# Two graph layers on one core: fewer maxima chunks, more differences on POOL, edge flags on DVE, the output bias in PE's sums

## Chip, cores and metric

The kernel runs on one core of one Trainium2 chip. The metric is the time of one execution of the whole program in microseconds (us). Before the change three runs gave a median of 1157.24 us (1155.14 to 1157.57).

## What is computed

x is (64 graphs, 128 nodes, 128 channels), adj is (64, 128, 128). Two residual layers follow each other; cut to what matters:

```python
h = relu(layernorm(x))
D = abs(h[:, :, None, :] - h[:, None, :, :])            # every pair of nodes of a graph
p = einsum('bijc,oc->bijo', D, W1) + b1                  # 64 products for each pair
p = leaky((p - mean(p)) / sqrt(var(p) + EPS) * g1 + be1) # statistics over all graphs and pairs
s = where(adj > 0, einsum('bijo,uo->biju', p, W2)[..., 0] + b2, NEG)
y = (softmax(s) @ h) @ Wg.T + bg
y = leaky((y - mean(y)) / sqrt(var(y) + EPS) * gg + beg) # again over all graphs
x = x + concatenate([h, y], axis=2) @ Wt.T + bt
h = relu(layernorm(x)); v = h @ W
e = leaky(v @ a[:128] + (v @ a[128:]).T, 0.2)
x = x + elu(softmax(where(adj > 0, e, NEG), axis=1) @ v)
```

## The kernel before

The pair differences need statistics over all graphs before they can be used, so the kernel goes through them twice. The 64 graphs are 32 couples of two, 16 quads of four. D is symmetric: 64 shifts of a graph against itself cover all pairs. A couple has 64 shifts in 8 chunks m = 0 to 7 of 8 shifts (PER = 8, CHUNKS = 256). Every engine has its program written out by hand, as a loop over a step n (chunk number) with offsets that say at which n each piece of work stands; an engine executes in that order and waits on semaphores.

**First pass** (about 30 to 660 us). For each chunk a tile `diff` of 128 x 2048 is made (5 slots, so chunk n waits for the product of chunk n-5). There are three sorts. In MAXED chunks (m = 0, 3, 6) DVE writes the maximum of the two nodes (`subtract` at L291, from PSUM and `h_ext`) and PE subtracts the sum of the two with twelve extra bf16 matmuls (`products_by_max`, L751 and L755): no absolute value is needed. In POOLED chunks (m = 1, 4, 7) POOL subtracts (L291), in the others (2, 5) DVE does; then ACT takes the absolute value (`absolute`, L567) and PE multiplies (`products`, L741). The products lie in one of three PSUM pairs of banks. KEPT chunks (all but m = 2, 7) are copied by ACT to SBUF (`take`) and stored in DRAM by SP's queue. The statistics of COUNTED chunks are made by DVE (`count`, bn_stats, L1040), from SBUF for kept ones and from PSUM for m = 2 and 7. For TAKEN chunks (m = 0, 5) ACT makes them: the copy with a running sum (L582) and a square from PSUM (L586). ACT's order in step n is: `normalise` and the other layer-norm pieces of the next quad (once a quad, at NORM_AT = 3, EXT_AT = 5, HIGH_AT = 7, MID_AT = 10), then `absolute(n)`, then `take(n-2)`. PE's transposes of the next quad stand at TURN_AT = 4, ahead of chunk 4 of the quad (L713); ACT's `turn_out` (L536) needs them. PE's `node_products` (NODE_AT = 6, L731) feed ACT's `high` (L541), whose rest DVE splits in `rest` and `low` (L1005, two inputs in SBUF). POOL also turns adj into flags `no_edge` (`edges`, L448, two halves for each couple).

**Second pass** (665 to 1003 us). SP loads the kept products into 10 slots (`load_kept`), chunks m = 2 and 7 are made again by DVE (`again`: L291 and a bit mask, L1055) and PE; ACT applies scale, bias and leaky relu (`activate`, L644), and PE sums the 64 products to scores (L845). Beside this runs the attention of quad j, at steps 16 j + offset: EVAC 24 `take_rows` (DVE), DIST_T 25 transposes (PE), TURN 27 `take_turned` (DVE), `store_skew`, `load_half` (DMAs through DRAM on POOL's queue, L470, L476) and `sum_half` (POOL, L480), SUM 41 `att_sum` (PE, L874, L875), SCORES 43 `att_scores` (DVE), EXP 45 (ACT, L649), NORM 48 `att_norm` (DVE, L1160), TURN_P 49 (PE), COPY 51 (DVE), MIX 53 (PE, L889), and Y 56 `att_y` (DVE: bias from PSUM, L1170, then bn_stats, L1171). `att_sum(j)` waits in `at_zero` for the y of quad j-1.

**The end of the second pass.** The last two quads' attention runs out with no chunks beside it. In this stretch SP loads x again (`load_x`, L383), POOL adds the bias of the output (`x_and_bias`, L485: six tiles between `load_half(15)` and `sum_half(15)`, ten behind it), and PE and DVE make the part of the output that comes from h for the first PRE = 6 quads (`outputs_of_x`, L799, at MADE_AT; `fold_x`, L1177, at FOLD_AT). Then come the statistics of y and the **last stage** (1050 us on), 16 quads in a software pipeline, with `outputs` (L915, L916) first.

Of the kernel before, what the change touches and what calls it, by code (L numbers as in the profile page):

```python
# [9 lines left out]
BF16 = mybir.dt.bfloat16  # L10
# [30 lines left out]
MAXED = (0, 3, 6)  # L41
POOLED = (1, 4, 7)
PLAIN = (2, 7)
COUNTED = (1, 2, 3, 4, 6, 7)
# [16 lines left out]
SUM_PARTS = (0, 16, 29, COUPLES)  # L61
# [25 lines left out]
def two_layers(nc, x, adj, adj_t, w1_tt, wg_t, wt1_t, wt2_t, l1_w, l1_wt, cols, bt_rows,  # L87
# [8 lines left out]
    with ExitStack() as ctx:  # L96
# [15 lines left out]
        bt_sb = sb("bt_sb", [128, C])  # L112
        ident = sb("ident", [128, 128])
# [34 lines left out]
        def by_graph(t):  # L148
# [9 lines left out]

        ln_st = sb("ln_st", [128, B, 6])
# [8 lines left out]
        sums_dump = sb("sums_dump", [128, NCOUNTED * 4])  # L168
# [39 lines left out]
        skew_stored = [sem("skew_stored0"), sem("skew_stored1")]  # L208
        skew_cleared = [sem("skew_cleared0"), sem("skew_cleared1")]
# [4 lines left out]
        weighted, weighted_ready = sem("weighted"), sem("weighted_ready")  # L214
# [4 lines left out]
        bt_ready, x_bt, y_act, o_mm, x1_ready, dve_f, var2_ready, rstd2_ready, scale2_ready, h2_ready, h2_turned, \  # L219
            h2t_ready = (sem(n) for n in (  # L220
                "bt_ready", "x_bt", "y_act", "o_mm", "x1_ready", "dve_f", "var2_ready", "rstd2_ready",
# [73 lines left out]
        EVAC, DIST_T, TURN, SUM, SCORES, EXP, NORM, TURN_P, COPY, MIX, Y = 24, 25, 27, 41, 43, 45, 48, 49, 51, 53, 56  # L295
        STORE_SKEW, LOAD_HALF = 30, 36
# [7 lines left out]
        def mix_at(n):  # L304
            u, r = divmod(2 * n, 3)
            return EARLY_MIX + u if r < 2 and 0 <= u < NQ - EARLY_MIX else None

# [11 lines left out]
        FOLD_AT = tuple(QCH * j + step for j in (NQ - 2, NQ - 1) for step in (SCORES, NORM, COPY))  # L319
        MADE_AT = (264, 266, 270, 274, 277, 284)  # L320
# [26 lines left out]
        def _(sp):  # L347
# [3 lines left out]
            def load_adj(v):  # L351

                if v >= 2:
                    sp.wait_ge(edges_set, 2 * (v - 1))
                sp.dma_start(adj_sb[v % 2], (adj_n, adj_tn)[v % 2][:, quad(v // 2), :]).then_inc(adj_in[v % 2], 16)
# [22 lines left out]
            def load_x(j):  # L378
                if j < PRE:
                    sp.wait_ge(prod2_ready, NPLAIN)  # L380
                else:
                    sp.wait_ge(scored, CHUNKS // 2)
                sp.dma_start(X[j], x_n[:, quad(j), :]).then_inc(x_in2[j], 16)  # L383

            AHEAD = LRING
            FIRST_LOADS = (LRING - 1) // len(KEPT) * PER + KEPT[(LRING - 1) % len(KEPT)]
            for n in range(CHUNKS + TAIL + AHEAD):
                if n < CHUNKS and n % PER in KEPT:
                    load_kept(n)
# [6 lines left out]
                if n == CHUNKS + AHEAD - 1:  # L396
                    for q in range(NQ):
                        load_x(q)
# [12 lines left out]
        def _(pool):  # L411
# [3 lines left out]
            nc.gpsimd.memset(skew_init[:, :], 0.0)  # L415
            nc.gpsimd.memset(sums_st[:, :, :], 0.0)
# [28 lines left out]
            def edges(v, half):  # L445
                pool.wait_ge(adj_in[v % 2], 16 * (v // 2 + 1))
                b = QUAD * (v // 2) + 2 * half
                nc.gpsimd.tensor_scalar(no_edge[v % 2][:, b:b + 2, :], adj_sb[v % 2][:, 2 * half:2 * half + 2, :], 0.0, None,  # L448
                                        ALU.is_le).then_inc(edges_set, 1)

            for n in range(CHUNKS):
# [4 lines left out]
                if n % PER in (2, 5):  # L456
                    edges(n // PER, n % PER // 5)
# [4 lines left out]
            def store_skew(j):  # L462
# [5 lines left out]
                whole = skew_dram[j % 2]  # L468
                dst = bass.AP(whole.tensor, whole.offset + 1, [[EXT + 1, N], [N * EXT, QUAD], [1, DIST]])
                nc.gpsimd.dma_start(dst, s_turn[:, :, :]).then_inc(skew_stored[j % 2], 16)  # L470
# [7 lines left out]
            def sum_half(j):  # L478
                pool.wait_ge(half_in, 16 * (j + 1))
                nc.gpsimd.tensor_tensor(s_half[:, :, 0:EXT - N], s_half[:, :, 0:EXT - N], s_half[:, :, N:EXT],  # L480
                                        ALU.add).then_inc(half_summed, 1)

            def x_and_bias(j):
# [819 lines left out]
```

## Time and profile before

| | |
|---|---|
| median of three runs | 1157.24 us (1155.14 to 1157.57) |
| the profiled execution's own time | 1156.38 us |
| its span in the trace | 1154.6 us |
| busy, share of the span | PE 91%, DVE 91%, ACT 86%, POOL 50% |
| first pass | to about 660 us |
| second pass | 665 to 1003 us |
| run-out of the attention | to about 1050 us |
| last stage | to 1154.6 us |

Busy times of an engine are unions: an instruction's last tenth of a microsecond overlaps the next one's start, so the distance of two starts is a little shorter than the duration shown. "Idle before" names what ended the wait of the engine. PEclk is the granted clock, 1.00 being 2.4 GHz and 0.50 being 1.2 GHz.

### The profile page before, as it was taken

Reading aid. Unit: us, or ns where it says so; the run is one execution under the profiler, and the core shown is the slowest. Engines: PE = TensorE matmul, PEld = TensorE weight load, DVE = VectorE, ACT = ScalarE, POOL = GpSimd, SP = SyncE. Lnnn points to the kernel's source line nnn. Section 1 sums busy time; section 2 is a strip of 40 time slices with the busy share of each in tenths; the row PEclk is TensorE's granted clock in tenths of the full one; section 3 lists DMA queues with packets and bytes.
Section 4 is the critical chain, followed back from the end, with each engine's and each line's share of the span. In section 5 each row is a group of like instructions: output and inputs, shape, how many; then the busy total and the mean of one; then the engine's idle time right before and its main releaser. Section 6 shows DMA issues by size and latency. Waiting matters only on the chain.

```text
span 1154.6 us, 17648 instructions
## 1 busy us (share of the span) xinstructions
PE 1054.3 (91%) x6470; PEld 473.9 (41%) x6470; DVE 1047.1 (91%) x1389; ACT 993.4 (86%) x1252; POOL 580.9 (50%) x332
## 2 busy tenths in 40 slices
PE   3999999999999999999999999999999999835997
PEld 1333333333333433333333452333333333335997
DVE  5999999999999999999999867999999999755887
ACT  4889998999999999999999889989899898703987
POOL 6587768767777877686777400111212221171330
PEclk9999999999999999999999989999999999976999
DMA  6444444444443444444444688999899999730012
GB/s 178 165 156 184 172 158 169 184 166 188 166 192 146 174 185 171 159 185 184 171 168 176 235 321 292 335 332 339 319 339 329 321 334 324 222 92 1 29 47 74
DMA packets 97269, 233.32 MB, mean 202 GB/s; under 512 B 8096, under 2 KB 44448, under 8 KB 97184
## 3 DMA queue, kind: packets, MB, share of 16 engines
q1 hardware_dynamic: 93040, 223.11, 53.2%
q0 software_dynamic: 2560, 8.39, 2.1%
q8 instruction: 52, 0.85, 0.3%
q10 hardware_dynamic: 1584, 0.69, 0.3%
q14 instruction: 33, 0.27, 0.1%
HBM read 124.43 MB, written 107.74 MB: 201 GB/s over the span
## 4 chain that ended last, share of the span: by engine, by line
PE 47%; DVE 37%; issue 7%; ACT 7%; DMA 1%; POOL 1%; ACTq 0%; DVEq 0%; POOLq 0%
PE psum L741 16%; DVE store L291 16%; PE psum L751 10%; PE psum L755 7%; DVE plain_st L1040 5%; DVE store L1055 4%; ACT store L567 3%; PE psum L932 1%; PE psum L916 1%; PE psum L933 1%; DVE early L1160 1%; PE psum L731 1%; PE psum L950 1%; PE psum L941 1%; PE psum L713 1%
## 5 line engine op out<-in xcount | busy, mean ns | idle before, releaser
L291 POOL TENSOR_TENSOR store<-h_ext 128x2048 f32<-128x2048 f32 (+1 forms) x96 | 386.6, 4029 | 119.5 <-PE psum L741 115.6
L741 PE MATMUL psum<-store,w1tt_sb 128*64 128x512 f32 x1792 | 421.1, 598 | 17.7 <-ACT store L567 17.5
L291 DVE TENSOR_TENSOR store<-psum,h_ext 128x2048 f32<-128x2048 f32 x160 | 364.1, 2275 | 0.7 <-ACT h_ext L537 0.7
L567 ACT ACTIVATE store<-store 128x2048 f32<-128x2048 f32 x160 | 305.1, 1932 | 6.2 <-POOL store L291 3.1
L644 ACT ACTIVATE store<-store,st 128x1024 f32<-128x1024 f32 x192 | 226.5, 1241 | 0.0
L741 PEld LDWEIGHTS psum<-store,w1tt_sb 128*64 128x64 f32 x1792 | 122.0, 136 | 252.8 <-issue 236.2
L751 PE MATMUL psum<-store,w_twice 128*64 128x512 f32 x768 | 200.6, 599 | 4.9 <-DVE early L1005 3.5
L291 DVE TENSOR_TENSOR store<-h_ext 128x2048 f32<-128x2048 f32 x64 | 146.2, 2285 | 17.9 <-PE psum L741 17.9
L1040 DVE BATCH_NORM_STATS2 plain_st<-store 128x6 f32<-128x512 f32 x256 | 160.6, 678 | 0.0
L755 PE MATMUL psum<-early 128*64 128x512 bf16 x1152 | 158.0, 380 | 0.0
L845 PE MATMUL psum<-store,w_rows 128*32 128x512 f32 x1024 | 134.3, 607 | 3.2 <-ACT store L644 3.2
L579 ACT COPY store<-psum 128x1024 f32<-128x1024 f32 x128 | 128.7, 1024 | 4.8 <-PE psum L741 4.8
L755 PEld LDWEIGHTS psum<-early 128*64 128x64 bf16 x1152 | 69.1, 110 | 133.0 <-issue 114.6
L1040 DVE BATCH_NORM_STATS2 plain_st<-psum 128x6 f32<-128x512 f32 x128 | 82.5, 686 | 17.9 <-PE psum L741 17.9
L1055 DVE TENSOR_SCALAR store<-store 128x2048 int32<-128x2048 int32 x64 | 81.3, 1270 | 2.2
L751 PEld LDWEIGHTS psum<-store,w_twice 128*64 128x64 f32 x768 | 53.0, 137 | 73.1 <-issue 29.1
L644 ACT ACTIVATE store<-psum,st 128x1024 f32<-128x1024 f32 x64 | 76.7, 1199 | 0.3 <-PE psum L741 0.3
L470 POOL DMA_DIRECT2D score_skew<-early x16 | 12.9, 805 | 120.2 <-DVE early L1133 120.2
L586 ACT ACTIVATE psum<-psum,st 128x1024 f32<-128x1024 f32 x64 | 69.8, 1091 | 1.1 <-DVE st L1084 1.1
L649 ACT ACTIVATE early<-early 128x512 f32<-128x512 f32 x16 | 10.1, 630 | 65.2 <-DVE early L1153 65.2
L582 ACT ACTIVATE store<-psum 128x1024 f32<-128x1024 f32 x64 | 65.4, 1022 | 0.2
L480 POOL TENSOR_TENSOR early<-early 128x256 f32<-128x256 f32 x16 | 17.1, 1070 | 92.5 <-DMA early<-score_skew 92.5
(155 smaller groups left out, 1195.6 us busy)
## 6 DMA issues: line engine op xcount, KB each, us to landing
kept_products<-store SPq DMA_DIRECT2D x192, 512.0 KB, 2.7
store<-kept_products SPq DMA_DIRECT2D x192, 512.0 KB, 6.0
early<-score_skew POOLq DMA_DIRECT2D x16, 384.0 KB, 6.8
early<-adj SPq DMA_DIRECT2D x16, 256.0 KB, 3.6
early<-adj_t SPq DMA_DIRECT2D x16, 256.0 KB, 3.5
store<-x SPq DMA_DIRECT2D x16, 256.0 KB, 5.6
out<-early SPq DMA_DIRECT2D x16, 256.0 KB, 2.3
score_skew<-early POOLq DMA_DIRECT2D x16, 128.0 KB, 6.0
```

Of the source, the lines that this page charges most:

```text
L291: return engine.tensor_tensor(t[:, :, 0:steps, :], nodes.unsqueeze(2).broadcast_to([C, 2, steps, N]), windows(h_ext[:, 2 * c, :], STEP * m ...
L567: nc.scalar.activation(t, t, ACT.Abs).then_inc(abs_ready, 1)
L579: nc.scalar.copy(kept[k % ZRING], tile).then_inc(kept_ready, 1)
L582: nc.scalar.activation(kept[k % ZRING], tile, ACT.Identity, accum_out=sum_p[:, t:t + 1])\
L586: nc.scalar.activation(tile, tile, ACT.Square, bias=sc(0), accum_out=sum_m[:, t:t + 1])\
L644: nc.scalar.activation(dst, src, ACT.Prelu, bias=sc(14), scale=sc(12), alpha=SLOPE0)\
L741: last = nc.tensor.matmul(t[MID * g:MID * g + MID, b, :], w1tt_sb[:, 0:MID], diff[slot][:, g, b * BANK:b * BANK + BANK], start=True, stop= ...
L751: nc.tensor.matmul(t[MID * g:MID * g + MID, b, :], w1_twice[:, :], diff[n % SLOTS][:, g, b * BANK:b * BANK + BANK], start=True, stop=False)
L755: last = nc.tensor.matmul(t[MID * g:MID * g + MID, b, :], y_parts[:, c % 4, s, MID * g:MID * g + MID], pair_nodes[:, k, b * BANK:b * BANK ...
L845: last = nc.tensor.matmul(score[j % 2][32 * q:32 * q + 32, :], w2_rows[:, r, :], src[:, b * BANK:b * BANK + BANK], start=(r == 0), stop=(r ...
L1040: last = nc.vector.bn_stats(plain_st[:, p, t, :], src[:, t, :])
L1055: nc.vector.tensor_scalar(bits, bits, 0x7FFFFFFF, None, ALU.bitwise_and).then_inc(diff2_ready, 1)
```

## The change

- First pass: MAXED is (0, 4), POOLED (1, 3, 5, 7), DVE's differences are m = 2 and 6, COUNTED is all but m = 0, so TAKEN is m = 0 alone. The offsets of the layer-norm pieces stay.
- `edges` goes from POOL (two halves) to DVE (one instruction a couple, ahead of the work of step m = 3).
- The output bias: DVE splits bt - 1 into three bf16 rows once, at step 32 (`split_bias`, eight small instructions), and PE adds it with one bf16 matmul of 512 columns for each quad (`biases`). POOL's sixteen `x_and_bias` are gone.
- x is loaded again by ACT's queue: eight issues between `activate(254)` and `activate(255)`, eight behind a wait for the last scores.
- PRE goes from 6 to 8; `outputs_of_x` stands at 257, 258, 266, 267, 270, 273, 277, 282, `fold_x` at new steps.
- `att_y` is cut in two: ACT adds the bias (`y_to_nodes`, step 56), DVE makes bn_stats (`y_sums`, step 57).
- The skewed store and load of quads 14 and 15 are issued by SP instead of POOL.
- The sums of the statistics (`sums`) take 224 instead of 192 chunks' values, cut at couples 16 and 27 instead of 16 and 29.

```diff
-MAXED = (0, 3, 6)
-POOLED = (1, 4, 7)
+MAXED = (0, 4)
+POOLED = (1, 3, 5, 7)
 PLAIN = (2, 7)
-COUNTED = (1, 2, 3, 4, 6, 7)
+COUNTED = (1, 2, 3, 4, 5, 6, 7)
...
-SUM_PARTS = (0, 16, 29, COUPLES)
+SUM_PARTS = (0, 16, 27, COUPLES)
...
-        FOLD_AT = tuple(QCH * j + step for j in (NQ - 2, NQ - 1) for step in (SCORES, NORM, COPY))
-        MADE_AT = (264, 266, 270, 274, 277, 284)
+        FOLD_AT = [QCH * (NQ - 1) + TURN] * 2 + [QCH * (NQ - 2) + step for step in (SCORES + 1, NORM, COPY, Y_SUMS)] + \
+            [QCH * (NQ - 1) + step for step in (SCORES, NORM)]
+        MADE_AT = (257, 258, 266, 267, 270, 273, 277, 282)
...
+            for j in range(BY_POOL, NQ):
+                store_skew(j)
+                load_half(j)
...
             for n in range(CHUNKS):
                 if n in POWER_AT:
                     deviation(POWER_AT.index(n))
                 if n % PER in POOLED:
                     differences(n)
-                if n % PER in (2, 5):
-                    edges(n // PER, n % PER // 5)
...
-                if j == NQ - 1:
-                    pool.wait_ge(bt_ready, 1)
-                    for q in range(PRE):
-                        x_and_bias(q)
                 sum_half(j)
...
-            for q in range(PRE, NQ):
-                x_and_bias(q)
...
+            def y_to_nodes(j):
+                act.wait_ge(out_mm, j + 1)
+                nc.scalar.activation(h_nat[:, quad(j), :], att[0], ACT.Identity, bias=BG).then_inc(y_out, 1)
...
                 if n < CHUNKS:
                     activate(n)
+                if n == CHUNKS - 2:
+                    act.wait_ge(prod2_ready, NPLAIN)
+                    for q in range(8):
+                        load_x(q)
+                if n == CHUNKS - 1:
+                    act.wait_ge(scored, CHUNKS // 2)
+                    for q in range(8, NQ):
+                        load_x(q)
...
+            def biases(o):
+                nc.tensor.matmul(o, ones_bf[:, :], bt_rows3[:, :].unsqueeze(1).broadcast_to([128, QUAD, C]),
+                                 start=True, stop=False)
...
-                for s, step in ((s_masked, SCORES), (y_ready, Y)):
+                for s, step in ((s_masked, SCORES), (y_out, Y)):
...
+            def edges(v):
+                dve.wait_ge(adj_in[v % 2], 16 * (v // 2 + 1))
+                nc.vector.tensor_scalar(no_edge[v % 2][:, quad(v // 2), :], adj_sb[v % 2], 0.0, None, ALU.is_le)\
+                  .then_inc(edges_set, 1)
...
+                in_turn(nc.vector.tensor_scalar(bt_sb[:, :], bt_sb[:, :], -1.0, None, ALU.add))
+                for k in range(2):
+                    in_turn(nc.vector.tensor_copy(bt_high[:, k, :], bt_sb[:, :]))
+                    in_turn(nc.vector.tensor_tensor(bt_sb[:, :], bt_sb[:, :], bt_high[:, k, :], ALU.subtract))
+                nc.vector.tensor_copy(bt_rows3[0:1, :], bt_high[0:1, 0, :])
+                nc.vector.tensor_copy(bt_rows3[32:33, :], bt_high[32:33, 1, :])
+                nc.vector.tensor_copy(bt_rows3[64:65, :], bt_sb[64:65, :]).then_inc(bt_ready, 1)
...
+                if n == 2 * QCH:
+                    split_bias()
+                if n < CHUNKS and n % PER == 3:
+                    edges(n // PER)
...
-            def att_y(j):
-                dve.wait_ge(out_mm, j + 1)
-                y = h_nat[:, quad(j), :]
-                linked(nc.vector.tensor_scalar(y, att[0], BG, None, ALU.add))
-                nc.vector.bn_stats(bst[:, j, :], y.rearrange("p b n -> p (b n)")).then_inc(y_ready, 1)
-
-            dve.wait_ge(edges_set, 2 * COUPLES)
+            def y_sums(j):
+                dve.wait_ge(y_out, j + 1)
+                nc.vector.bn_stats(bst[:, j, :], h_nat[:, quad(j), :].rearrange("p b n -> p (b n)")).then_inc(y_ready, 1)
```

## Rows read from the trace of the kernel before

**Rows 1.** Stretches: busy us (instructions) of PE, PEld, DVE, ACT, POOL; PEclk; DMA share, GB/s.
```profile
100.00:500.00 400.00, 388.18 (x2184) 151.27 (x2182) 387.70 (x419) 375.63 (x430) 296.39 (x143) 1.00 0.45 174
...
800.00:1000.00 200.00, 187.61 (x1236) 67.58 (x1232) 194.97 (x213) 179.11 (x165) 41.35 (x37) 1.00 0.90 320
1000.00:1050.00 50.00, 22.32 (x148) 17.83 (x144) 27.05 (x40) 4.25 (x6) 24.30 (x22) 0.75 0.39 103
```

**Rows 2.** One POOL instruction of each couple's chunk 7: count, first and last start.
```profile
L289 POOL TENSOR_TENSOR store<-h_ext x32: 453/457/461, 31.8 to 645.9; 128x128 f32<-128x128 f32 x32
```

**Rows 3.** Groups by line in 100 to 500 us.
```profile
L291 POOL TENSOR_TENSOR store<-h_ext 128x2048 f32<-128x2048 f32 (+1 forms) x61 | 245.9, 4032 | 75.6 <-PE psum L741 75.6
...
L1040 DVE BATCH_NORM_STATS2 plain_st<-store 128x6 f32<-128x512 f32 x163 | 102.3, 678 | 0.0
```

**Rows 4.** Timeline of the first pass: start, duration, engine, line.
```profile
299.95 1.03 PE L751 MATMUL psum<-store,w_twice 128*64 128x512 f32 x4
...
301.17 1.02 ACT L582 ACTIVATE store<-psum 128x1024 f32<-128x1024 f32 x1
...
302.96 1.89 PE L741 MATMUL psum<-store,w1tt_sb 128*64 128x512 f32 x8
...
303.25 1.02 ACT L579 COPY store<-psum 128x1024 f32<-128x1024 f32 x1
...
304.14 3.74 ACT L567 ACTIVATE store<-store 128x2048 f32<-128x2048 f32 x2
...
314.23 0.66 PE L713 MATMUL psum<-ident,h_nat 128*128 128x128 f32 x4
...
314.93 0.59 ACT L536 COPY h_ext<-psum 128x512 f32<-128x512 f32 x1 [0.58 <-PE psum L713]
```

**Rows 5.** Waits of ACT in 100 to 500 us: total, times, longest.
```profile
ACT early L541 <- PE psum L731: 13.4, 10, 1.3
ACT h_ext L536 <- PE psum L713: 4.6, 8, 0.6
```

**Rows 6.** DVE beside POOL: one stretch of the timeline, and two lines' durations.
```profile
376.21 8.01 POOL L291 TENSOR_TENSOR store<-h_ext 128x1792 f32<-128x1792 f32 x2
...
378.76 1.38 DVE L1005 TENSOR_TENSOR early<-y_rest,early 128x256 bf16<-128x256 f32 x1
...
L1005 DVE TENSOR_TENSOR early<-y_rest,early x16: 400/408/1383, 22.0 to 613.6; 128x256 bf16<-128x256 f32 x16
...
L1055 DVE TENSOR_SCALAR store<-store x64: 1226/1227/1737, 655.4 to 991.4; 128x2048 int32<-128x2048 int32 x64
```

**Rows 7.** DVE's bias of y in the second pass: durations, first and last start.
```profile
L1170 DVE TENSOR_SCALAR h_nat<-psum,col x16: 739/744/751, 743.6 to 1046.2; 128x512 f32<-128x512 f32 x16
```

**Rows 8.** SP's loads of x: duration of the issue, min/median/max in ns.
```profile
L383 SPq DMA_DIRECT2D store<-x x16: 383/832/1791, 1000.6 to 1013.1; - x16
```

**Rows 9.** Timeline from the last activation to the second batch-norm.
```profile
1001.55 1.19 ACT L644 ACTIVATE store<-psum,st 128x1024 f32<-128x1024 f32 x1
...
1010.22 0.78 POOL L470 DMA_DIRECT2D score_skew<-early  x1 [4.30 <-DVE early L1133]
...
1010.89 1.95 PE L799 MATMUL psum<-wt_sb,h_ext 128*128 128x128 f32 x16
...
1013.26 0.63 ACT L649 ACTIVATE early<-early 128x512 f32<-128x512 f32 x1 [10.52 <-DVE early L1153]
...
1017.88 0.76 POOL L476 DMA_DIRECT2D early<-score_skew  x1 [6.88 <-issue]
1018.65 7.35 POOL L485 TENSOR_TENSOR store<-store,bt_sb 128x512 f32<-128x512 f32 x6
...
1021.55 5.00 DVE L1160 TENSOR_TENSOR early<-early,rows 128x512 f32<-128x512 f32 x1
...
1034.28 0.46 PE L874 MATMUL psum<-early,ident 128*128 128x128 f32 x2 [1.67 <-DVE bst L1171]
...
1037.78 2.14 DVE L1153 TENSOR_TENSOR early<-early,rows 128x512 f32<-128x512 f32 x1
```

More of the change, by code:

```diff
@@ L208, in two_layers @@
         skew_stored = [sem("skew_stored0"), sem("skew_stored1")]
+        late_stored, late_in = ([sem(f"{t}{n}") for n in range(2)] for t in ("late_stored", "late_in"))
         skew_cleared = [sem("skew_cleared0"), sem("skew_cleared1")]
@@ L306, in mix_at, with skewed @@
             return EARLY_MIX + u if r < 2 and 0 <= u < NQ - EARLY_MIX else None
+        BY_POOL = NQ - 2
+        def skewed(j):
+            whole = skew_dram[j % 2]
+            return bass.AP(whole.tensor, whole.offset + 1, [[EXT + 1, N], [N * EXT, QUAD], [1, DIST]])
         def quad_at(n, step):
@@ L376, in load_kept, with store_skew, load_half @@
                 sp.dma_start(loaded[k % LRING], kept_dram[k, :, :]).then_inc(kept_in[k % LRING], 16)
[L378 to L385, printed above, removed]
+            def store_skew(j):
+                sp.wait_ge(turn_ready, j + 1)
+                sp.wait_ge(half_in, 16 * (j - 1))
+                sp.dma_start(skewed(j), s_turn[:, :, :]).then_inc(late_stored[j - BY_POOL], 16)
+            def load_half(j):
+                sp.wait_ge(late_stored[j - BY_POOL], 16)
+                sp.wait_ge(s_sum, j)
+                sp.dma_start(s_half[:, :, :], skew_dram[j % 2].rearrange("b (i j) -> i b j", j=EXT))\
+                  .then_inc(late_in[j - BY_POOL], 16)
             FIRST_LOADS = (LRING - 1) // len(KEPT) * PER + KEPT[(LRING - 1) % len(KEPT)]
-            for n in range(CHUNKS + TAIL + AHEAD):
-                if n < CHUNKS and n % PER in KEPT:
+            for n in range(CHUNKS):
+                if n % PER in KEPT:
                     load_kept(n)
@@ L597, in sums @@
                                                      (1, ACT.Identity, dict(scale=256.0)))):
-                    at = 4 * first + (1024 if k == 1 else 0)
-                    dump = (sums_dump[:, :] if k == 2 else tiles(28, 4))[:, at:at + 4 * (last - first)]
+                    dump = sums_dump[k][part][:, 0:4 * (last - first)]
                     done = nc.scalar.activation(dump, counted_part(of)[:, 4 * first:4 * last], how,
@@ L653, in _ @@
                     activate(n)
+                if n == CHUNKS - 2:
[6 more added lines that the diff above has]
+                        load_x(q)
                 if mix_at(n) is not None:
                     nodes_out(mix_at(n))
[L656 to L658 removed]
+                for step, do in ((Y, y_to_nodes), (EXP, exps)):
+                    j = quad_at(n, step)
+                    if j is not None:
+                        do(j)
             def bn_leaky(j):
@@ L1181, in _ @@
                     again(n + LEAD_DIFF)
-                for step, do in ((Y, att_y), (EVAC, take_rows), (TURN, take_turned), (SCORES, att_scores),
+                for step, do in ((Y_SUMS, y_sums), (EVAC, take_rows), (TURN, take_turned), (SCORES, att_scores),
                                  (NORM, att_norm), (COPY, att_copy)):
@@ L1186, in _ @@
                         do(j)
-                if n in FOLD_AT:
-                    fold_x(FOLD_AT.index(n))
+                for k in range(PRE):
+                    if n == FOLD_AT[k]:
+                        fold_x(k)
             done[0] = 0
```

83 lines of the change are left out of this document (47 added, 36 removed).

## The prediction

> **What bounds the kernel now.** I read the busy times by stretch first, then, in the first pass, the period of a couple, the groups, ACT's waits and a piece of the timeline; in the second pass DVE's lines; behind it the timeline. From 100 to 500 us DVE is busy for 387.7 us of 400, PE for 388.2, ACT for 375.6, POOL for 296.4 [rows 1]. The same instruction of POOL comes every (645.9 - 31.8) / 31 = 19.81 us [rows 2]: that is a couple; a quad takes 39.6 us, and 400 us hold 10.1 quads. A quad so has 38.4 us of DVE, 38.4 of PE, 37.2 of ACT, 29.3 of POOL. Three engines are within 6% of the bound, so taking work from one helps only as far as the next, and ACT is that next one. In the second pass (800 to 1000 us) DVE is busy for 97.5%, PE for 94%, ACT for 89.6% [rows 1]: DVE ends it. In the run-out (1000 to 1050 us) no engine is busy for more than 27 of 50 us: a chain of waits.
>
> **First pass: PE.** Two maxima chunks a quad become chunks of differences. A maxima chunk starts at 299.95 and the next one at 302.96, 3.0 us; a chunk of differences takes up to 1.9 [rows 4]. PE loses at least 2.2 us a quad and bounds nothing any more.
>
> **DVE.** Per couple it loses one difference (2.2) and gets one pair of bn_stats (2 x 0.61, as 102.3 us for 163 give 0.63 [rows 3]) and one `edges`. No row has this instruction on DVE. Bounds: a quarter of the 2048-wide one, 0.31, and the 512-wide one from PSUM, 0.74 [rows 6, 7]; I take 0.5. 19.2 - 2.2 + 1.2 + 0.5 = 18.7 us a couple, 37.4 a quad.
>
> **POOL.** Four differences of 4.0 us (245.9 / 61 [rows 3]) and about 0.4 more for chunk 7, 33.5 us a quad: free, unless a difference starts late.
>
> **ACT.** Per quad two absolute values more, 2 x 1.87 (3.74 for two [rows 4]); two chunks are copied only: from L582's start at 301.17 to L579's at 303.25 are 2.08 us, a copy takes 0.9 (303.25 to 304.14) [rows 4], so 2 x 1.2 less. 37.2 + 3.7 - 2.4 = 38.5 us. To this comes a wait that the new order makes. `turn_out` stands ahead of `absolute(5)` and needs the transposes that PE does behind chunk 3. Before, ACT had `absolute(4)` to do meanwhile and waited 0.58 us [rows 4], in all 4.6 us in 400 [rows 5]. Now m = 4 is a maxima chunk and m = 2 isn't kept, so between `absolute(3)` and `turn_out` ACT has only the copy of chunk 1, 0.9 us, while PE does chunk 3, which waits for that absolute value (1.8), and 0.70 us from the transposes' start to ACT's [rows 4]: a wait of 1.6 us in each quad that no lead of PE can hide. The wait for `node_products` (13.4 us in 400 [rows 5]) should mostly go: two absolute values of ACT now stand behind PE's chunk 5 by my working of the order. So a quad takes at least 38.5 + 1.6 = 40.1 us, and I take 40.3, with 0.2 for the waits that remain: 0.7 more than 39.6, in 15.5 quads **+11 us**. From both sides: 39.7 (all small waits gone, the added wait half hidden) is +1, and 40.9 (0.8 of the old waits kept) is +20.
>
> **DVE and POOL together.** `low` (L1005, both inputs in SBUF) takes 0.41 us, but 1.38 where it meets a running difference of POOL: at 378.76 it lasts until 380.14, shortly behind the end (379.9) of the first of POOL's two differences [rows 6]. `split_bias` has two such subtractions and other small instructions beside them. If each subtraction and copy waits for the rest of a difference of 4.0 us, half of it on average, that is 4 x 2 = 8 us of DVE once, of which the other engines' lead hides most: **+2** (0 to +8). `edges` has one input in SBUF; a mask with one input (L1055) takes 1.23 and at most 1.74 in a pass in which POOL does little [rows 6], so I let `edges` wait only where DVE has room for it (18.7 of 20.2 us a couple).
>
> The Trainium skill (SBUF — State Buffer, Who interferes with whom) says that `tensor_scalar` from SBUF to SBUF can also take the port pair that POOL uses, and that the later of the two then waits for the whole instruction. The trace agrees for two inputs and shows no certain case for one. By that rule the second rival below is the likelier course; by the rows alone the sum stands.
>
> **Second pass.** The bias of y leaves DVE: 16 x 0.744 us [rows 7], of which some twelve lie where DVE is the bound, 9 us. ACT gets as much (0.6 to 0.74 each) and goes from 89.6% of a quad of 21.1 us (338 us for sixteen) to 96% of one of 20.3: nearly a bound. Its waits leave DVE part of the gain: **-7** (-9 to -1).
>
> **The run-out.** First a loss: eight DMA issues now stand between `activate(254)` and `activate(255)`, which started at 1001.55 [rows 9], with the last scores behind it. An issue of this load took 0.38 to 1.79 us on SP, median 0.83, most of that under a full queue [rows 8]; for the first eight I take 0.55: +4.4 (3.1 to 6.7). Two `outputs_of_x` of 1.0 us (1.95 for two [rows 9]) plus a bias matmul now stand ahead of quad 13's end; ACT's bias beside `take_rows` gives about as much back. So quad 14's exponential ends at 1013.9 + 4.4, about 1018.3, instead of 1013.9 [rows 9]. Then the gain. Before, DVE sat behind `fold_x(0)`, this behind POOL's `x_and_bias`, this behind the issue at 1017.88, which waited 7.7 us for the store of 1010.22 [rows 9]; and the normalising L1160 then took 5.00 us beside POOL's six, until 1026.55 [rows 9]. Now three folds (0.7 each) and 1.6 us of normalising follow: 1021.5. On to `att_sum(15)` were 7.7 us, to 1034.28 [rows 9]; without the four `outputs_of_x` between them at half clock about 5: 1026.5. The half of quad 15 is stored at about 1014 and, with 7.7 us for the store as before, 4.8 for the load and 0.7 for the sum, there at 1027.2; without the queue of x earlier. So 1027 against 1034.3, -7.3; L1153's 2.14 us beside POOL [rows 9] are 0.7 again, -1.4: **-9** (-14 to -3).
>
> **Last stage.** Two quads less of eight matmuls (0.12 us each, as sixteen in 1.95 [rows 9]), eight bias matmuls more: 0. `sums`: 0. POOL makes one pair table less ahead of the first chunks: 0 to -1.
>
> **Sum.** The profiled execution has 1156.4 us; + 11 + 2 - 7 - 9 = 1153.4. The median of the runs is 0.9 above it, so 1154.
>
> **Rivals.** *The shared wait* (slower): in each couple `edges` meets a difference of POOL that has just begun. Its place is step m = 3; its price is up to 4.0 us for DVE, and it decides from the point where it exceeds DVE's room, 20.2 - 18.7 = 1.5 us. At 4.0 in each second couple, 16 x 2.5 = 40; at an average rest of 2.0 in all, 32 x 0.5 = 16. I take +22: 1176. For it: L1005's 1.38, and POOL now has a difference on for 83% of the time. Against it: L1005 met one seldom (median 0.408 [rows 6]), as the order puts it into POOL's pauses. Chance 0.22.
> *The ACT wait doesn't come* or old waits shrink as much (39.6 us a quad, PE's room helps all): first pass 0 instead of +11, so 1143. For it: PE gets 2.2 us of air; against it: chunk 3 needs `absolute(3)`. Chance 0.17.
> *The end gives less*: ACT becomes the bound of the second pass (-2) and the eight issues cost 6.7 and more, the skews come no sooner (-4): 1164. Chance 0.13.
> *Forecast*, 1154 (1146 to 1162): 0.48.
>
> **Numbers.** About 0.2% (2.3 us) is what a measurement can tell. Of the forecast's 0.48, 0.28 lies more than 2.3 under 1157.2, 0.15 within, 0.05 above; of the ACT rival's 0.17, 0.15 is faster and 0.02 within; of the other two's 0.35, 0.32 is slower and 0.03 within. Faster 0.43, same 0.20, slower 0.37. The range leaves out 2 in 10: 1142 to 1179, from the ACT rival to the shared wait's mean with its spread.
>
> **What would show it.** The pass-1 instruction of POOL in chunk 7 comes every 20.15 us; L536's counterpart on ACT waits about 1.6 us in each quad; ACT is busy 96% there, PE under 90%. `edges` lasts 0.3 to 0.7 us; durations of 2 to 4 us there mean the shared wait. The y line on DVE is gone and DVE's share falls from 97.5%. Eight issues between the last two activations take 4 to 5 us; from the first of them to `att_sum(15)` pass about 25.5 us, where from the same place (1001.55) to 1034.28 it was 32.7. A first pass of 19.8 us a couple or less makes the forecast wrong, as does a run-out that isn't shorter.

## The result, and the profile after

The changed kernel takes 1188.39 us, the median of four runs (1187.35 to 1190.48), against 1156.19 (1154.60 to 1157.57) for the kernel before beside it: a ratio of 1.0276, interval 1.0251 to 1.0300. It is 32 us slower, and outside the range of 1142 to 1179. The profiled execution took 1187.45 us, its span is 1185.5.

The stretches below are divided by these landmarks, which both kernels have: `turn_out`'s copies in the first pass (ACT, one a quad, L537 now), the first and last but one activation of the second pass, and the first batch-norm output `bn_leaky`.

| stretch | before | after | difference |
|---|---|---|---|
| start to the second quad's copy | 36.54 | 44.58 | +8.0 |
| from there to the sixteenth copy, 14 quads | 554.97 | 589.90 | +34.9 |
| to the first activation of the second pass | 71.95 | 76.40 | +4.4 |
| to `activate(254)` | 336.96 | 329.16 | -7.8 |
| run-out, to `bn_leaky` | 49.33 | 40.41 | -8.9 |
| last stage | 104.85 | 105.05 | +0.2 |

So the three stretches behind the first pass came out as forecast in their sums, and the first pass with its two ends lost 47 us instead of 13. Busy times by stretch in the kernel after (columns as in [rows 1]; the third row has the length of one whole quad, the last is 2 us at the start of a chunk 3):

```profile
100.00:500.00 400.00, 353.17 (x1852) 137.58 (x1850) 378.68 (x450) 369.14 (x369) 330.92 (x118) 0.98 0.43 167
800.00:1000.00 200.00, 190.83 (x1264) 68.59 (x1260) 195.45 (x208) 188.25 (x177) 39.57 (x37) 1.00 0.94 336
258.54:298.82 40.28, 35.97 (x194) 14.08 (x192) 37.04 (x42) 38.02 (x38) 33.66 (x13) 1.00 0.44 170
338.00:340.00 2.00, 2.00 (x7) 0.60 (x4) 2.00 (x3) 0.29 (x1) 2.00 (x1) 0.50 0.44 180
```

In the first pass no engine is as full as PE and DVE were in [rows 1]. The POOL instruction of [rows 2], `edges` (L1075) and `low` (L1035) by source line, then ACT's waits from 100 to 500 us:

```profile
L293 POOL TENSOR_TENSOR store<-h_ext x32: 449/460/656, 39.0 to 688.3; 128x128 f32<-128x128 f32 x32
L1075 DVE TENSOR_SCALAR no_edge<-early x32: 400/414/4526, 35.7 to 684.1; 128x512 uint8<-128x512 int32 x32
L1035 DVE TENSOR_TENSOR early<-y_rest,early x16: 417/668/2945, 23.1 to 656.0; 128x256 bf16<-128x256 f32 x16
```

```profile
PE psum L762 <- ACT store L568: 46.5, 31, 3.7
ACT h_ext L537 <- PE psum L734: 21.0, 9, 3.5
```

The couple now comes every (688.3 - 39.0) / 31 = 20.95 us. The wait at `turn_out` was 4.6 us in 400 [rows 5] and is 21.0. The timeline shows what it consists of, once in a regular quad, the length that recurs most (first two lines: its chunk 3 and its copy), and once in a long one:

```profile
297.26 1.94 PE L762 MATMUL psum<-store,w1tt_sb 128*64 128x512 f32 x8 [2.29 <-ACT store L568]
...
299.82 0.59 ACT L537 COPY h_ext<-psum 128x512 f32<-128x512 f32 x1 [1.81 <-PE psum L734]
...
335.49 1.90 ACT L568 ACTIVATE store<-store 128x2048 f32<-128x2048 f32 x1
337.29 1.00 ACT L580 COPY store<-psum 128x1024 f32<-128x1024 f32 x1
337.54 3.54 PE L762 MATMUL psum<-store,w1tt_sb 128*64 128x512 f32 x8 [2.29 <-ACT store L568]
341.01 0.70 PE L734 MATMUL psum<-ident,h_nat 128*128 128x128 f32 x4
341.74 0.59 ACT L537 COPY h_ext<-psum 128x512 f32<-128x512 f32 x1 [3.46 <-PE psum L734]
```

Six of the fourteen quads take 40.28 or 40.29 us and have the wait of 1.81. Three take 41.9: there PE stood idle for 2.29 us for `absolute(3)`, the granted clock from 338 to 340 us is 0.50, so 1.2 GHz, and the eight matmuls of chunk 3 take 3.54 us instead of the 1.9 of [rows 4]. ACT waits 3.46 us. In the regular quads PE stands idle there for the same 2.29 us (first line), and the clock stays at 1.00. The other five take 41.1 to 48.2; the half clock lies in some of them too (in the one that ends at 219.26, behind an idle time of PE of 3.49 us).

Two more losses lie at the ends. At the start POOL's first difference began just ahead of a small instruction of DVE, which then took 3.68 us instead of 0.20, and a second one met the next difference. In the kernel before the first difference began only at 17.09: POOL's third pair table had held up a small instruction of DVE (L995, 2.13 us at 11.07 instead of 0.16), and with it ACT's first copy. And half of `edges` had stood ahead of POOL's second difference, so that the second small instruction (L995 again) came through in 0.36 us. At the end of the pass the last `edges` took 4.53 us. DVE and POOL at the start in the kernel before (first two lines), then in the kernel after:

```profile
23.24 0.85 POOL L448 TENSOR_SCALAR no_edge<-early 128x256 uint8<-128x256 int32 x1
23.28 0.36 DVE L995 SCALAR_TENSOR_TENSOR ln<-ln 128x4 f32<-128x4 f32 x1 [0.92 <-POOL ln L428]
...
15.42 3.68 DVE L1043 TENSOR_SCALAR w_twice<-w1tt_sb 128x64 f32<-128x64 f32 x1 [4.42 <-DMA fold<-fold_in]
...
24.40 4.18 POOL L295 TENSOR_TENSOR store<-h_ext 128x2048 f32<-128x2048 f32 x1
24.45 4.14 DVE L1025 SCALAR_TENSOR_TENSOR ln<-ln 128x4 f32<-128x4 f32 x1 [0.90 <-POOL ln L444]
...
679.85 8.36 POOL L295 TENSOR_TENSOR store<-h_ext 128x2048 f32<-128x2048 f32 x2
...
684.11 4.53 DVE L1075 TENSOR_SCALAR no_edge<-early 128x512 uint8<-128x512 int32 x1
```

The run-out, to be read beside [rows 9]:

```profile
1040.21 5.69 ACTq L653 DMA_DIRECT2D store<-x  x8
1046.01 1.20 ACT L649 ACTIVATE store<-psum,st 128x1024 f32<-128x1024 f32 x1 [4.74 <-issue]
1049.26 5.13 ACTq L653 DMA_DIRECT2D store<-x  x8
1054.44 0.69 ACT L657 ACTIVATE h_nat<-psum,col 128x512 f32<-128x512 f32 x1 [7.23 <-PE psum L916]
```

### The profile page after: what moved, and what is told of

Same layout as the page of the kernel before. It is cut to its first block, busy times and chain, and to the rows that moved or that the text cites. A ratio compares the mean times of both kernels' runs of the same rounds, so it can differ in the third digit from the quotient of the medians.

```text
span 1185.5 us, 16875 instructions
## 1 busy us (share of the span) xinstructions
PE 1034.8 (87%) x6102; PEld 464.2 (39%) x6102; DVE 1051.0 (89%) x1446; ACT 1020.6 (86%) x1204; POOL 636.5 (54%) x281
## 4 chain that ended last, share of the span: by engine, by line
ACT 34%; DVE 27%; PE 26%; issue 11%; ACTq 1%; POOL 1%; DMA 0%; DVEq 0%; POOLq 0%
ACT store L568 13%; DVE store L295 10%; PE psum L762 9%; ACT store L649 8%; DVE plain_st L1070 6%; ACT store L580 5%; PE psum L872 3%; ACT psum L587 2%; PE psum L772 2%; ACT store L583 2%; ACT h_nat L530 2%; PE psum L776 1%; PE psum L734 1%; PE psum L980 1%; DVE store L1107 1%
## 5 line engine op out<-in xcount | busy, mean ns | idle before, releaser
L295 POOL TENSOR_TENSOR store<-h_ext 128x2048 f32<-128x2048 f32 (+1 forms) x128 | 521.7, 4089 | 114.9 <-PE psum L776 104.6
L762 PE MATMUL psum<-store,w1tt_sb 128*64 128x512 f32 x2048 | 495.6, 614 | 77.0 <-ACT store L568 77.0
L568 ACT ACTIVATE store<-store 128x2048 f32<-128x2048 f32 x192 | 371.6, 1944 | 17.5 <-DVE store L295 15.9
L295 DVE TENSOR_TENSOR store<-psum,h_ext 128x2048 f32<-128x2048 f32 x128 | 290.9, 2273 | 3.5 <-PE psum L762 3.5
L762 PEld LDWEIGHTS psum<-store,w1tt_sb 128*64 128x64 f32 x2048 | 147.8, 139 | 364.0 <-issue 330.1
L1070 DVE BATCH_NORM_STATS2 plain_st<-store 128x6 f32<-128x512 f32 x320 | 202.1, 676 | 34.5 <-ACT store L580 34.5
L580 ACT COPY store<-psum 128x1024 f32<-128x1024 f32 x160 | 161.0, 1032 | 7.3 <-PE psum L776 6.3
L295 DVE TENSOR_TENSOR store<-h_ext 128x2048 f32<-128x2048 f32 x64 | 146.5, 2288 | 17.0 <-PE psum L762 16.9
L772 PE MATMUL psum<-store,w_twice 128*64 128x512 f32 x512 | 136.7, 608 | 8.8 <-DVE early L1035 6.4
L776 PE MATMUL psum<-early 128*64 128x512 bf16 x768 | 107.3, 383 | 0.0
L872 PEld LDWEIGHTS psum<-store,w_rows 128*32 128x32 f32 x1024 | 21.7, 108 | 76.0 <-ACT store L649 50.4
L537 ACT COPY h_ext<-psum 128x512 f32<-128x512 f32 x16 | 9.4, 586 | 39.9 <-PE psum L734 39.9
```

Source lines behind the costliest of these rows:

```text
L295: return engine.tensor_tensor(t[:, :, 0:steps, :], nodes.unsqueeze(2).broadcast_to([C, 2, steps, N]), windows(h_ext[:, 2 * c, :], STEP * m ...
L568: nc.scalar.activation(t, t, ACT.Abs).then_inc(abs_ready, 1)
L580: nc.scalar.copy(kept[k % ZRING], tile).then_inc(kept_ready, 1)
L762: last = nc.tensor.matmul(t[MID * g:MID * g + MID, b, :], w1tt_sb[:, 0:MID], diff[slot][:, g, b * BANK:b * BANK + BANK], start=True, stop= ...
L772: nc.tensor.matmul(t[MID * g:MID * g + MID, b, :], w1_twice[:, :], diff[n % SLOTS][:, g, b * BANK:b * BANK + BANK], start=True, stop=False)
L776: last = nc.tensor.matmul(t[MID * g:MID * g + MID, b, :], y_parts[:, c % 4, s, MID * g:MID * g + MID], pair_nodes[:, k, b * BANK:b * BANK ...
```

## The experiments

Two theories for the first pass: the wait that the new order makes at `turn_out` (with the half clock behind it), and the shared wait of DVE's small instructions for POOL's differences. Each kernel is a short edit of the kernel after, and the kernel before ran beside it (median 1153.8 to 1155.2 on these chips, 1156.2 beside the kernel after; so a difference between the median of an experiment and that of the kernel after can be off by 1 to 2.4 us).

**TURN_AT 3.** The copies stand one step sooner, so that ACT has the next absolute value behind them.

```diff
-NORM_AT, TURN_AT, EXT_AT, ... = 3, 4, 5, ...
+NORM_AT, TURN_AT, EXT_AT, ... = 3, 3, 5, ...
```

> The changed kernel with PE's transposes of the next quad ahead of chunk 3 instead of chunk 4 (TURN_AT 3). Theory W (the loss of the first pass is ACT's wait for transposes that stand behind chunk 3, 1.81 us and more in each quad, plus the halved clock of chunk 3 that follows PE's own idle time): turn_out no longer waits, a regular quad falls from 40.28 to 38.6 to 38.9 us, and the time to 1155 to 1164 us. Theory S (the loss is DVE waiting for POOL's running differences): nothing of that moves, the time stays above 1180 us.

1181.60 us, 1.0239 (1.0222 to 1.0255). The wait at `turn_out` was gone and the regular quad took 39.27 us, as in the kernel before, but five others took 44 to 46. The median `edges` went from 414 to 979 ns, and single ones cost a whole difference (`edges` by source line; timeline):

```profile
L1075 DVE TENSOR_SCALAR no_edge<-early x32: 406/979/4535, 35.2 to 677.9; 128x512 uint8<-128x512 int32 x32
...
140.58 4.19 POOL L295 TENSOR_TENSOR store<-h_ext 128x2048 f32<-128x2048 f32 x1 [1.24 <-PE psum L776]
141.04 4.15 DVE L1075 TENSOR_SCALAR no_edge<-early 128x512 uint8<-128x512 int32 x1
```

Each theory was half right: with one wait away, the other took most of its place.

**Edges on POOL.** Two halves a couple on POOL, as before the change; the rest as changed.

```diff
+                if n % PER in (2, 5):
+                    edges(n // PER, n % PER // 5)
-                if n < CHUNKS and n % PER == 3:
-                    edges(n // PER)
```

> The changed kernel with the edge flags back on POOL in two halves. Theory W: regular quads stay at 40.28 us, only the few long ones lose something: 1180 to 1190 us (POOL gets 3.4 us a quad more and may make a difference late). Theory S: the stalls of DVE go, the time falls by 20 us and more, under 1168 us.

1190.63 us, 1.0312 (1.0279 to 1.0344): nothing gained. Two things lie in this. From 220 us on its ten quads are as long as those of the kernel after, within 0.05 us. And ahead of that the start gained 8.7 us, but the third quad took 52.4 us instead of 41.1, since a copy of one row in `split_bias` (4.14 us) and `low` (4.30 us) met differences there. The regular quads stayed at 40.28 with the wait of 1.81, and the shared wait moved to `low` (L1042 here), whose median went from 668 ns to 1484. The start did recover, with the second copy at 35.84: the first small instruction came first this time, and the second one found POOL waiting for its `edges`.

```profile
13.71 0.19 DVE L1050 TENSOR_SCALAR w_twice<-w1tt_sb 128x64 f32<-128x64 f32 x1 [2.66 <-DMA fold<-fold_in]
...
14.93 4.18 POOL L295 TENSOR_TENSOR store<-h_ext 128x2048 f32<-128x2048 f32 x1 [4.08 <-ACT h_ext L545]
...
L1042 DVE TENSOR_TENSOR early<-y_rest,early x16: 417/1484/4297, 19.8 to 657.2; 128x256 bf16<-128x256 f32 x16
```

**The old order of chunks, edges on DVE.**

```diff
-MAXED = (0, 4)
-POOLED = (1, 3, 5, 7)
-COUNTED = (1, 2, 3, 4, 5, 6, 7)
+MAXED = (0, 3, 6)
+POOLED = (1, 4, 7)
+COUNTED = (1, 2, 3, 4, 6, 7)
```

> The changed kernel with the mix of chunks of before (maxima in three, POOL in three, squares by ACT in two), all else as changed, the edge flags on DVE too. Theory W: the added wait goes, DVE bounds again with 0.8 us a quad more than before for the flags: first pass 10 to 16 us longer than before, run-out and second pass shorter by 12: 1154 to 1162 us. Theory S: the flags alone cost DVE 2 us and more in each couple: over 1170 us.

1206.69 us, 1.0466 (1.0439 to 1.0493): slower still. In every second couple `edges` met a difference that had begun 1.2 us before, and `low` met another (timeline):

```profile
272.85 4.20 POOL L295 TENSOR_TENSOR store<-h_ext 128x2048 f32<-128x2048 f32 x1 [4.27 <-PE psum L762]
274.02 3.32 DVE L1075 TENSOR_SCALAR no_edge<-early 128x512 uint8<-128x512 int32 x1
...
285.46 4.21 POOL L295 TENSOR_TENSOR store<-h_ext 128x2048 f32<-128x2048 f32 x1 [1.96 <-PE psum L762]
287.43 2.53 DVE L1035 TENSOR_TENSOR early<-y_rest,early 128x256 bf16<-128x256 f32 x1
```

Both end 0.29 us behind POOL's end (274.02 + 3.32 = 277.34 against 277.05; 289.96 against 289.67). The quad was 42.79 us.

**A filled PE.** Sixteen bf16 matmuls whose results are overwritten stand on PE ahead of each quad's chunk 3, so that PE isn't idle there.

```diff
+                if n % QCH == 3 and n > 3:
+                    for g in range(16):
+                        nc.tensor.matmul(prod[n % 3][...], y_parts[...], pair_nodes[:, 0, 0:BANK], start=True, stop=True)
```

> The changed kernel with sixteen bf16 matmuls (about 1.7 us, results overwritten) on PE where it waits for the absolute value of chunk 3, once a quad from the second quad on. Theory W with the clock in it: PE stays at 1.00 there, turn_out waits 1.81 us in every quad, the quads of 41.9 us go to 40.28 and the very long ones lose 1.6 us: 1176 to 1182 us. If the clock isn't part of it: 1187 to 1190 us, unchanged.

1174.03 us, 1.0167 (1.0144 to 1.0189), 14 us less for more work. In a regular quad chunk 3 has PE idle for 0.47 us, runs at the full clock, and from the fourth copy on every `turn_out` waits 1.72 (timeline):

```profile
331.18 1.90 PE L798 MATMUL psum<-early 128*64 128x512 bf16 x16
333.55 1.94 PE L762 MATMUL psum<-store,w1tt_sb 128*64 128x512 f32 x8 [0.47 <-ACT store L568]
...
336.11 0.59 ACT L537 COPY h_ext<-psum 128x512 f32<-128x512 f32 x1 [1.72 <-PE psum L734]
```

The quads of 41.9 us are gone; three of 43 to 47 stay. Between the two profiles 10.3 us lie in the fourteen quads and 4 at the end of the pass, where the last `edges` took 1.01 us instead of 4.53. So I put the half clock itself at about 10 us, an estimate; 1.4 of them are 0.1 us in every quad (a regular one takes 40.18 instead of 40.28), which the clock doesn't explain.

**x behind the activations.** The first eight loads are issued with the other eight.

```diff
-                if n == CHUNKS - 2:
+                if n == CHUNKS - 1:
                     act.wait_ge(prod2_ready, NPLAIN)
```

> The kernel after with its first eight loads of x issued on ACT behind the last activation of pass 2 (with the other eight) instead of ahead of it. In the kernel after the eight cost ACT 4.7 us between activate(254) and activate(255), with the last plain chunk and att_sum(15) behind them. If the run-out is a chain through activate(255), as the prediction's sum had it, this gives 4 to 5 us: 1183 to 1185. Rival: ACT's issues are only moved, and sixteen in a row then delay what ACT does between activate(255) and bn_leaky (y of quads 13 and 14, exps): 1187 to 1190.

1187.47 us (1185.68 to 1189.03), 1.0283: the rival's outcome. The run-out took 41.3 us, against 40.4. Why, the last experiment takes up.

**TURN_AT 3, edges on POOL, x behind the activations**, the three edits above together.

> Three edits at once in the kernel after: TURN_AT at 3, edges on POOL again (two halves a couple, as before the change), x issued behind the last activation. Theory (each of two limits took the other's place: ACT waits at turn_out for PE with TURN_AT 4, DVE waits for POOL's running differences with TURN_AT 3): with edges off DVE the regular quad is 38.5 to 39.3 us and the first pass ends 15 to 25 us sooner than in the kernel after, so 1150 to 1165. Rival: with TURN_AT 3 the limit is the ring behind POOL's own work (four differences, and two halves of edges a couple, 34.5 us of 39.3), or chunk 3's half clock stays as after: quads of 40 us or more and 1170 to 1182.

1166.13 us (1161.53 to 1168.47), 1.0099 (1.0067 to 1.0131). The first part alone had given 7 us and the other two nothing; together they give 22 (20, if each kernel is set against the kernel before beside it). The gain lies in the first pass: its end, the first activation, comes at 685.4 instead of 710.9, and of these 25 us 10.9 lie at the start and 14.3 in the fourteen quads. The second pass and the run-out are within 1 us of the kernel after, so the place of x has no part in it. The regular quad is 39.27, no less. The third quad took 50.9 us: two small instructions of DVE met differences there, the first of them a plain copy of one row in `split_bias`.

```profile
102.39 4.20 POOL L295 TENSOR_TENSOR store<-h_ext 128x2048 f32<-128x2048 f32 x1 [1.18 <-PE psum L782]
102.51 4.13 DVE L1097 COPY bt_rows<-bt_high 1x128 bf16<-1x128 bf16 x1
...
107.38 4.17 POOL L295 TENSOR_TENSOR store<-h_ext 128x2048 f32<-128x2048 f32 x1
107.53 4.30 DVE L1041 TENSOR_TENSOR early<-y_rest,early 128x256 bf16<-128x256 f32 x1
```

**The old order, edges on POOL.** The first pass as before the change but for `split_bias`; all the rest as changed.

> Pass 1 as before the change (chunks of maxima 0, 3, 6, POOL's differences 1, 4, 7, edges on POOL), with all the rest of the change kept: bias in PE's sums, y copied by ACT, last two skews on SP, x loaded on ACT's queue, seven statistics. Theory: the whole loss is the first pass's new order of chunks, and what the other parts give is the run-out's 8.9 us and pass 2's 2.8: 1156 minus 9 to 12, 1144 to 1148. Rival 1: part of the first pass's loss is not the chunks' (split_bias on DVE, POOL's first difference 2 us sooner, which strikes DVE's first instructions, the longer statistics): 1149 to 1156. Rival 2: the gain of pass 2 comes from the chunks' order too: 1147 to 1149.

1148.47 us (1144.37 to 1151.01, eight runs), 0.9949 (0.9933 to 0.9966). This is the change without its new first pass, and it is faster than the kernel before. Against the run with the old order and edges on DVE, which differs in `edges` alone, it is 58 us faster: 3.6 us a quad for two instructions of 0.42.

**The same, x behind the activations.**

> The run before this one with the first eight loads of x behind the last activation. Theory: 4 to 5 us below that run, 1139 to 1143 if it stands at 1144 to 1148; the fastest so far. Rival: the sixteen issues in a row only move the wait: within 1 us of that run.

1147.30 us (1146.51 to 1148.76), 0.9942 (0.9920 to 0.9964): 1.2 us below the run before it, where the theory had 4 to 5 and the rival under 1. The difference is inside the spread of that run's executions.

**A guard at the start** of the kernel after: POOL's first difference waits until DVE has made the doubled weights.

```diff
+                if n == POOLED[0]:
+                    pool.wait_ge(weights_made, 1)
```

> The kernel after with one wait more: POOL's first difference waits until DVE has made the doubled weights (the small instruction that took 3.68 us in the kernel after because POOL's difference had begun 0.54 us before the weights landed, and 0.19 us in the runs where it came first). Theory: this lost race is the start's delay, about 8 us at the second quad: the doubled weights take 0.2 us, the second quad's copy stands at 36 to 39 us instead of 43.8 to 44.6, and the run takes 1180 to 1184. Rival: DVE's next small instructions meet the same or the next difference anyway (one took 4.14 us at 24.45), and the quad that is saved at the start comes back as a long quad later, as in the run with edges on POOL: 1186 to 1190.

1189.73 us, with a spread of 1181.45 to 1193.73: inconclusive in time. The instruction took 0.20 us, but in the profiled execution its weights landed only at 17.55, and the next collision came as before, so the second copy stood at 43.30:

```profile
17.55 0.20 DVE L1045 TENSOR_SCALAR w_twice<-w1tt_sb 128x64 f32<-128x64 f32 x1 [6.55 <-DMA fold<-fold_in]
...
24.00 4.14 DVE L1027 SCALAR_TENSOR_TENSOR ln<-ln 128x4 f32<-128x4 f32 x1 [0.90 <-POOL ln L444]
```

The rival for the start, one collision following the other, held. The other runs show what decides the second collision. In all six kernels with `edges` on DVE, the one with the old order of chunks among them, the small layer-norm instruction behind `deviation` took 4.13 or 4.14 us; in all eight with `edges` on POOL it took 0.16 to 0.37, as `edges` stood on POOL between `deviation` and the next difference. With the old order, where the doubled weights took 0.2 us either way, the second copy stood at 40.65 with `edges` on DVE and at 36.4 to 37.7 with them on POOL.

**The bias split between the passes.** Two kernels: the one with the three edits, and the one with the old order and edges on POOL.

```diff
-                if n == 2 * QCH:
-                    split_bias()
             nc.vector.tensor_copy(sc(19), sc(18)).then_inc(pass2_ready, 1)
+            split_bias()
```

> The run with TURN_AT 3, edges on POOL and x after the activations, with the bias split between the two passes (POOL stands still there) instead of inside the third quad of the first pass. In the run without this, the quad that held it took 50.9 us, with stalls of 4.13 us in the split and 4.30 us right behind it. Theory: that quad falls to 41 to 43 us and 2 us of DVE's work are added between the passes: 6 to 9 us less, 1157 to 1160. The regular quad stays at 39.27 us, since ACT is busy 38.0 of it and waits 1.26 for PE: the new order of chunks gives nothing over the old one even with these waits gone. Rival: the long quad is the coming of a shift in phase between POOL and DVE that happens with or without the split: 1163 to 1167.

> The run with the old order of chunks and edges on POOL (1148.5 us), with the bias split between the two passes instead of inside the first. In that run the split had one stall of 4.23 us and its quad took 43.74 us against 39.3 to 41 in the others. Theory: the first pass is 4 us shorter and the join 2 us longer at most: 1144 to 1146.5, the fastest of all. Rival: DVE's work at the join delays the second pass by as much, or the quad is long anyway: 1148 to 1150.

With the new order 1155.41 us (ten runs, 1153.42 to 1161.59), 1.0012 (0.9997 to 1.0027), 11 less: no measurable difference from the kernel before. With the old order **1143.79 us** (1142.07 to 1146.62), 0.9904 (0.9887 to 0.9922), 5 less and faster than both kernels of this case. The third quad fell from 50.9 to 40.96 and from 43.74 to 39.27 us. A regular quad by stretch, first in the kernel with the new order, with ACT's only two waits in it, then in the one with the old:

```profile
279.76:319.03 39.27, 35.89 (x195) 14.56 (x192) 36.26 (x39) 38.02 (x39) 36.73 (x17) 1.00 0.45 174
...
286.86 0.37 ACT L549 CAST early<-psum 128x256 bf16<-128x256 f32 x1 [0.81 <-PE psum L758]
304.54 1.01 ACT L587 COPY store<-psum 128x1024 f32<-128x1024 f32 x1 [0.44 <-PE psum L782]
```

```profile
276.75:316.03 39.28, 38.30 (x218) 14.86 (x220) 37.26 (x37) 36.98 (x42) 28.54 (x15) 1.00 0.45 174
```

38.02 + 0.81 + 0.44 = 39.27: ACT, with those two waits, is the bound of the new order. The old one ends at the same length with PE at 38.30. Even free of the waits for PE at `turn_out` and of `edges`, the new order moves the bound without lowering it.

**The second eight loads of x behind quad 13's y**, in the fastest kernel.

```diff
-                if n == CHUNKS - 1:
+                if n == QCH * (NQ - 3) + Y:      # behind y_to_nodes(13)
                     act.wait_ge(scored, CHUNKS // 2)
```

> The fastest kernel so far (old order of chunks, edges on POOL, bias split between the passes, 1143.8 us) with the second eight loads of x issued on ACT behind its copy of quad 13's y instead of ahead of it. Moving the first eight behind the last activation gave nothing in two kernels: quad 13's y stood behind all sixteen issues either way (1013.06 right behind the issues' end at 1013.01, and 1054.44 behind 1054.39 in the kernel after). Theory: the sixteen issues are on the chain through that y; with eight of them behind it, y comes 5 us sooner and the run-out is 4 to 5 us shorter: 1139 to 1140. Rival: quad 15's skew on SP, or the loads of x that now come later, take its place: 1142 to 1145.

1143.66 us (1141.74 to 1146.15), 0.9911 (0.9895 to 0.9927): nothing. The y came 1.4 us sooner, not 5, since it now waited for PE, and quad 14's exponential then waited for the issues (timeline):

```profile
1007.73 0.69 ACT L664 ACTIVATE h_nat<-psum,col 128x512 f32<-128x512 f32 x1 [6.65 <-PE psum L923]
1007.74 6.41 ACTq L660 DMA_DIRECT2D store<-x  x8
1014.19 0.63 ACT L668 ACTIVATE early<-early 128x512 f32<-128x512 f32 x1 [5.77 <-issue]
```

The sixteen issues keep ACT for 10.1 to 12.9 us in all, wherever they stand; whichever of y and the exponential comes next pays. The Trainium skill (DMA: Bandwidth & Descriptors, Issuing engines are not separate DMA queues) calls the time to initiate a DMA usually small relative to the DMA itself. In these traces it was 0.63 to 0.81 us of ACT a load in the mean of the sixteen, against a median of 5.0 to 5.6 us until a load has landed: small beside the load, but sixteen take a quarter or more of the run-out's 41 us.

## Why the prediction was wrong

The step that failed is the first pass, forecast at +13 and measured at +47: 34.9 us in fourteen quads, 8.0 at the start and 4.4 at the end. What the forecast of the quads left out is the half clock behind PE's idle time, and the time that DVE's small instructions wait for POOL. The sums for the second pass, the run-out and the last stage held. The medians of six kernels show the first pass in its parts (x's place, worth nothing, apart):

| order of chunks | `turn_out` at | edges on POOL | edges on DVE |
|---|---|---|---|
| old | 4 | 1148.5 | 1206.7 |
| new | 4 | 1190.6 | 1188.4 (the change) |
| new | 3 | 1166.1 | 1181.6 |

- **ACT's quad**, the step of +11: the regular quad was forecast at 40.3 us and took 40.28; ACT's work 38.5 and measured 38.02; its added wait 1.6 and measured 1.81. So the quad is right. What failed is the step from a quad to the pass: "40.3, with 0.2 for the waits that remain: 0.7 more than 39.6, in 15.5 quads". The 39.6 was a mean over long quads (41) and regular ones (39.28), the 40.3 a regular one, and the long quads were let grow by nothing. Against 39.28 the regular length alone gives 14 us in 14 quads; the long ones add 34.9 - 14 = 21.
- **The clock** is missing from the working of the first pass. The prediction had that PE "bounds nothing any more", and didn't ask what an idle PE costs. The 1.81 us were called a wait "that no lead of PE can hide", but their length counted on the full clock. The filled PE shows its size: about 10 us, 9 of them in the long quads.
- **DVE and POOL together**, the step of +2, and the rival of the shared wait. The sentence "I let `edges` wait only where DVE has room for it" fell: one input or two made no difference. The rival's mechanism and price (up to 4.0 us) were right, its role was not. In the old order, where DVE has no room, `edges` cost 58 us. In the new order taking it away alone gave nothing: ACT's wait at `turn_out` covered it in the regular quads, `low` met the differences in its place, and a long third quad ate the gain at the start. Both waits had to go for the 22 us. The Trainium skill (SBUF — State Buffer, Who interferes with whom) had said that `tensor_scalar`, `copy` and `cast` from SBUF to SBUF can meet this wait too; the trace agrees, with 3.32 against 0.42 us and 4.13 for a row of 128 values. The prediction gave this rule, its first rival (it calls it the second), a chance of 0.22 with a price for the mean; the better reading would have been two limits at once, neither of which shows while the other stands.
- **`split_bias`** was +2 (0 to +8): in the two kernels without ACT's wait its place in the first pass cost 11 and 5 us. In the kernel after its instructions happened to meet no difference.
- **The start** was given 0 to -1 and is +8, by two collisions. One pair table less let POOL's difference begin at 14.9 instead of 17.1, ahead of weights that DVE needed. And `edges`, gone from POOL, had kept POOL's second difference out of the way of a layer-norm instruction. The prediction counted what the removed work gave, not what it had kept back. Without the first collision (the guard) the second copy still stood at 43.3; in the three kernels with the new order and `edges` on POOL, where neither collision came, it stood at 33.7 to 35.8.
- **The end of the first pass** has another 4 to 5 us, the last `edges` at 684.11; with edges on POOL this stretch, counted from the last chunk 7, was 16.9 us instead of 22.0, before the change 17.1.
- **Second pass**: -7 forecast, -7.8 measured. DVE's share there didn't fall, as one of the signs had it: 195.45 us of 200, 97.7%. **Run-out**: -9 and -8.9. Eight issues ahead of `activate(255)`: 4.4 and 4.7; from the first of them to `att_sum(15)` 25.5 and 26.2. But that the "+4.4" act through `activate(255)` is refuted: moving the issues behind it gave nothing in two kernels. In all kernels the sixteen issues stand ahead of quad 13's y or quad 14's exponential, so what they cost the run-out is not shown, and the agreement of the sum is in part luck. **Last stage**: 0 and +0.2.
- Two sums of the working are a little off without bearing on the result: POOL's quad adds up to 2 x (4 x 4.0 + 0.4) = 32.8, not 33.5 (measured 33.66), and 1018.3 with three folds and 1.6 us gives 1022.0, not 1021.5.

Still open in part is why the new order, with `turn_out`'s wait gone, `edges` on POOL and the bias split between the passes, takes 11 us more of first pass than the old one (676.14 against 664.97 at the first activation) though the regular quads are equal. Of these, 9.7 lie in the long quads: its six take 41 to 43.3 us, the old order's four 40.4 to 41.1. The shared wait isn't gone there: `low` takes 1.38 to 2.98 us in fifteen of its sixteen places, in the old order 1.38 in two and 0.4 elsewhere, and a layer-norm instruction on 128 x 20 values takes 2.45 us in each of the two longest quads (42.8 and 43.3), in the old order 0.17. What each of these costs no run separates. Nor does a run take away the start's second collision alone.

## What to carry to other kernels

Ask of two near limits not which is the larger but what each hides: removing one alone gave 0 to 7 us here and both together 22. Ask of work that leaves an engine what its place in the order had kept apart: `edges` gone from POOL brought a difference ahead of a small instruction of DVE, 4.14 us instead of 0.36. Put small VectorE instructions between SBUF tensors, whatever their size, where GpSimd stands still (here between the passes, 5 to 11 us for eight instructions of 2 us). When work is taken off TensorE, look for the place where it now waits, since the chunk behind that place can run at half the clock.

## What the hardware showed unexpectedly

- A one-input instruction of DVE from SBUF to SBUF waits for a running two-input instruction of POOL to its end: 3.32 us instead of 0.42 (int32 to uint8), 4.13 for 1 x 128 bf16. DVE's differences with one input in PSUM stayed at 2.26 to 2.29 us, and a pair of bn_stats at 1.26 to 1.29, though POOL was busy for 33.66 of 40.28 us.
- PE's granted clock fell to 0.50 behind an idle time of 2.29 us in three quads, and stayed at 1.00 behind the same 2.29 us in the six regular quads. Where sixteen filler matmuls left 0.47, it stayed at 1.00. So the length of this one pause doesn't decide alone; what does is not shown.
